# A bidirectional selective-scan block on one core: projections of each pass, once a phase of their own, spread in pieces over the scan of the pass before

## What is computed

```python
h, gate = adaln(x, cond)                  # layernorm, then (1 + scale) and shift from cond @ w + b
xs, z = split(h @ in_w)                   # 256 -> 2 x 512
xs = silu(xs)
proj = xs @ xproj_w                       # 512 -> 512 + 64 + 64
dt = softplus(proj[:512] + dt_bias); B = proj[512:576]; C = proj[576:640]
A = -exp(A_log)
for t in range(256):
    hst = hst * exp(dt_t[:, None] * A) + (dt_t * xs_t)[:, None] * B_t[None, :]
    y_t = hst @ C_t
ssm = (y + xs * D) * silu(z) @ out_w
x = x + gate * (ssm_fwd + ssm_bwd)
x = x + gate2 * (silu(h2 @ w1) * (h2 @ w2) @ w3)      # h2 = adaln(x) again
```

## Time and profile before

| | |
|---|---|
| median of 3 runs | 5650.15 us |
| the profiled execution, its own time | 5651.32 us |
| its span, first to last instruction | 5649.6 us |
| mean granted TensorE clock | 0.986 |
| busy: PE / DVE / ScalarE (ACT) / POOL | 80% / 86% / 56% / 57% |
| projections | 0 to about 656 us |
| first scan starts, last one ends | 690.7, about 5187.5 us |

### The profile page before, as it was taken

How to read it: one execution, slowest core, us unless ns; L and a number is a source line. 1 busy time by engine, 2 the same in 40 slices (tenths; PEclk the granted TensorE clock), 3 DMA queues, 4 the chain that set the end, 5 groups by cost and what they waited for, 6 DMA issues and landing times. The chain is left out here.

```text
span 5649.6 us, 129100 instructions
## 1 busy us (share of the span) xinstructions
PE 4528.9 (80%) x44208; PEld 2356.7 (42%) x44208; DVE 4867.9 (86%) x2556; ACT 3161.1 (56%) x10364; POOL 3230.3 (57%) x6078
## 2 busy tenths in 40 slices
PE   8999677777777777777777777777777777776898
PEld 4445344444444444444444444444444444443444
DVE  2332499999999999999999999999999999997433
ACT  4665466666665666665656565656565656564121
POOL 0000176767676767676767676767676767674221
PEclk9999899999999999999999999999999999998899
DMA  4333201111111111111111111111111111112551
GB/s 136 130 112 137 94 26 28 29 29 28 29 28 28 28 28 28 28 28 28 28 28 28 28 28 28 28 28 28 28 28 28 28 30 28 28 28 71 163 156 63
DMA packets 394408, 273.65 MB, mean 48 GB/s; under 512 B 212416, under 2 KB 299968, under 8 KB 393792
## 3 DMA queue, kind: packets, MB, share of 16 engines
q1 hardware_dynamic: 389568, 261.61, 15.4%
q10 hardware_dynamic: 4224, 4.19, 0.2%
HBM read 154.24 MB, written 111.41 MB: 47 GB/s over the span
## 5 line engine op out<-in xcount | busy, mean ns | idle before, releaser
L808 DVE TENSOR_TENSOR_SCAN b_hs<-b_dA,b_u 128x1024 f32<-128x1024 f32 x2048 | 4484.4, 2269 | 20.4 <-PE b_u L831 9.3
L831 PE MATMUL b_u<-b_ud,b_bw 32*128 32x256 f32 x16384 | 2322.9, 399 | 971.5 <-ACT b_dA L744 854.7
L744 ACT ACTIVATE b_dA<-b_ex 128x496 f32<-128x496 f32 x4096 | 2282.8, 585 | 257.0 <-PE b_ex L841 255.2
L841 PE MATMUL b_ex<-b_dd,b_aw 32*128 32x512 f32 x8192 | 2349.9, 641 | 28.8 <-DVE b_aw L796 28.1
L831 PEld LDWEIGHTS b_u<-b_ud,b_bw 32*128 32x128 f32 x16384 | 1489.9, 184 | 1941.7 <-issue 961.1
L655 POOL TENSOR_TENSOR b_dd<-b_dr,b_mask 128x512 f32<-128x512 f32 x1024 | 1073.4, 1048 | 1207.1 <-DVE b_hs L808 1188.7
L861 PE MATMUL b_y<-b_hs,b_cw 128*32 128x256 f32 x16512 | 1293.0, 390 | 2.7 <-DVE b_hs L808 2.7
L759 ACT ACTIVATE b_u<-b_hin 128x32 f32<-128x32 f32 x1792 | 362.7, 202 | 1502.7 <-PE b_u L831 939.7
L664 POOL TENSOR_TENSOR b_ud<-b_ur,b_mask 128x512 f32<-128x512 f32 x1024 | 1082.5, 1057 | 0.0
L841 PEld LDWEIGHTS b_ex<-b_dd,b_aw 32*128 32x128 f32 x8192 | 649.4, 183 | 30.8 <-issue 28.5
L743 ACT ACTIVATE b_first<-b_ex 128x16 f32<-128x16 f32 x3584 | 630.7, 176 | 38.5 <-PE b_ex L841 33.5
(11 more groups left out here) (98 smaller groups left out, 1918.2 us busy)
## 6 DMA issues: line engine op xcount, KB each, us to landing
scratch_y<-b_ysb SPq DMA_DIRECT2D x129, 256.0 KB, 2.1
b_u<-scratch_ut SPq DMA_DIRECT2D x256, 128.0 KB, 2.9
scratch_xs<-a_xs SPq DMA_DIRECT2D x16, 1024.0 KB, 7.2
scratch_sz<-a_sz SPq DMA_DIRECT2D x16, 1024.0 KB, 8.8
scratch_dt<-a_dt SPq DMA_DIRECT2D x16, 1024.0 KB, 4.5
scratch_ut<-a_uT SPq DMA_DIRECT2D x16, 1024.0 KB, 7.9
b_ur<-scratch_ut SPq DMA_DIRECT2D x1024, 16.0 KB
b_dr<-scratch_dt SPq DMA_DIRECT2D x1024, 16.0 KB, 1.7
```

Of the source, the lines that this page charges most:

```text
L744: nc.scalar.activation(dA[:, j % NDA, h, :, 1:TC], src[:, :, 1:TC], ACT.Exp).then_inc(exp_done, 1)
L808: nc.vector.tensor_tensor_scan(hs[:, c % 2, v, :, :, kp].rearrange("p d t -> p (d t)"), dA[:, j % NDA, :, :, :].rearrange("p h d t -> p (h ...
L831: ins = nc.tensor.matmul(dst[:, :, tb, :], bw[row(r), c % 2, tb, :], ud[row(r), j // 2 % NPR, tb, :, :], start=(tb == 0), stop=(tb == NTB ...
L841: nc.tensor.matmul(e[bank_of(p, 2 * j + h)][:, :], aw[row(r), d, v, :, :].rearrange("p b s -> p (b s)"), dd[row(r), j // 2 % NPR, :, :].re ...
```

## The change

The first two phases become one, `main_phase`. The work of one pass is now a `unit(q)`: a Python generator on each engine, cut into pieces, which yields after each. Unit 0 runs whole before the scan. Unit p + 1 runs during pass p: PE takes one piece after each step, ScalarE one piece in each step from j = 3 on, POOL two in each pair from the third on, SP one group of stores and loads after the loads of each chunk but the first. `wait_steps(n)` leaves n steps without a piece, and so lines the engines up.

- There are two PSUM banks for exponents instead of three (NDT), since one bank (b_job) is now for the units. PE's wait for the bank stands ahead of each exponent matmul instead of ahead of the step.
- The states hs have one buffer instead of two; the add-up goes by half chunks (8 steps), each in the 8 steps after it, and read_y comes twice as often with half the width.
- Silu is made of Exp, Ln and Exp on ScalarE (x * exp(-ln(1 + exp(-x)))) with a clamp and a product on POOL; softplus' four DVE operations become two on ScalarE and three on POOL, the product u one more on POOL; normalising goes to POOL, the root is Ln and Exp. All functions come from one table set, loaded once. Of the units only bn_stats and bn_aggr stay on DVE.
- B and C are projected in one job, and B is then transposed. Weights are held for one direction at a time, and are loaded anew for each pass.

The diff, cut to its core:

```diff
-        NDA, NPR, NM, NDT = 4, 4, 4, 3
+        NDA, NPR, NM, NDT = 4, 4, 4, 2
-        hs = sb("b_hs", [P, 2, SPN, SD, TC, 2])
+        hs = sb("b_hs", [P, SPN, SD, TC, 2])
+        GROUP_AT = {1: (0,), 2: (1,), 3: (2,), 4: (3, 4), 5: (5,), 6: (6,), 7: (7,)}
+        SILUS = 2 * JB
+        DT_JOB = (8, 10, 13, 15)
+        UT_JOB = (11, 14, 16, 17)
+        BC_JOB, BT_JOB, UNIT_JOBS = 9, 12, 18
+        STAT_AT = {64: 0, 66: 1, 68: 2, 70: 3}
+        AGGR_AT = {72: 0, 74: 1, 76: 2, 78: 3}
...
@@ SP @@
+                        load(p, c)
+                        if p + 1 < PASSES:
+                            if c == 1:
+                                side = unit(p + 1)
+                            if c:
+                                next(side)
...
@@ POOL @@
+                def softplus(q, j):
+                    m = q * JB + j
+                    pool.wait_ge(logged, m + 1)
+                    nc.gpsimd.tensor_tensor(nd[:, :], wy[:, :], ey[:, :], ALU.subtract).then_inc(nd_made, 1)
+                    yield
+                    pool.wait_ge(nd_made, 2 * m + 1)
+                    nc.gpsimd.tensor_tensor(nd[:, :], ln[:, :], nd[:, :], ALU.subtract).then_inc(nd_made, 1)
+                    yield
+                    pool.wait_ge(nd_made, 2 * m + 2)
+                    pool.wait_ge(sz_stored[j], (q + 1) * 16)
+                    nc.gpsimd.tensor_tensor(sd[:, j, :], pre[:, :], nd[:, :], ALU.add).then_inc(dt_made, 1)
+                    yield
+                    pool.wait_ge(dt_made, m + 1)
+                    if j >= 2:
+                        pool.wait_ge(full, first_job(q) + UT_JOB[j - 2] + 1)
+                    nc.gpsimd.tensor_tensor(us[:, j % 2, :], sd[:, j, :], xs[:, j, :], ALU.mult).then_inc(u_made, 1)
+                    yield
+                def unit(q):
+                    for i in range(SILUS):
+                        clamp(q, i)
+                        yield from wait_steps(3)
+                        if i:
+                            times_sigmoid(q, i - 1)
+                        yield
+                    yield from wait_steps(4)
+                    times_sigmoid(q, SILUS - 1)
+                    yield from wait_steps(2)
+                    for j in range(JB):
+                        yield from softplus(q, j)
+                        yield from wait_steps((8, 10, 8, 12)[j])
...
@@ POOL, one_pass @@
                         if c:
                             carry_in(p, 2 * i)
+                        if i >= 2:
+                            next(side, None)
                         ahead(p, i + 1, turn_u, last)
...
                         if c:
                             carry_in(p, 2 * i + 1)
+                        if i >= 2:
+                            next(side, None)
...
@@ ScalarE @@
+                def sigmoid(q, i):
+                    m = q * SILUS + i
+                    both = cl[:, i % 2, :]
+                    act.wait_ge(clamped, m + 1)
+                    nc.scalar.activation(both, both, ACT.Exp, scale=-1.0).then_inc(chain, 1)
+                    yield
+                    act.wait_ge(chain, 3 * m + 1)
+                    nc.scalar.activation(both, both, ACT.Ln, bias=1.0).then_inc(chain, 1)
+                    yield
+                    act.wait_ge(chain, 3 * m + 2)
+                    nc.scalar.activation(both, both, ACT.Exp, scale=-1.0).then_inc(chain, 1)
...
+                def take_dt(q, j):
+                    m = q * JB + j
+                    n = first_job(q) + DT_JOB[j]
+                    bias = dtb[:, q % DIRS, j:j + 1]
+                    act.wait_ge(full, n + 1)
+                    if m:
+                        act.wait_ge(dt_made, m)
+                    nc.scalar.activation(pre[:, :], job_bank(n)[:, :], ACT.Relu, bias=bias)
+                    nc.scalar.activation(ey[:, :], job_bank(n)[:, :], ACT.Abs, bias=bias).then_inc(freed, 1)
+                def log_part(q, j):
+                    m = q * JB + j
+                    act.wait_ge(freed, first_job(q) + DT_JOB[j] + 1)
+                    nc.scalar.activation(ey[:, :], ey[:, :], ACT.Exp, scale=-1.0).then_inc(bent, 1)
+                    yield
+                    act.wait_ge(bent, 2 * m + 1)
+                    nc.scalar.activation(wy[:, :], ey[:, :], ACT.Identity, bias=1.0).then_inc(bent, 1)
+                    yield
+                    act.wait_ge(bent, 2 * m + 2)
+                    nc.scalar.activation(ln[:, :], wy[:, :], ACT.Ln)
+                    nc.scalar.activation(wy[:, :], wy[:, :], ACT.Identity, bias=less[:, :]).then_inc(logged, 1)
...
+                def unit(q):
+                    for i in range(SILUS):
+                        take_xz(q, i)
+                        yield
+                        if i:
+                            yield from sigmoid(q, i - 1)
+                        else:
+                            yield from wait_steps(2)
+                        yield
+                    take_dt(q, 0)
+                    yield
+                    yield from sigmoid(q, SILUS - 1)
+                    yield
+                    yield from log_part(q, 0)
+                    take_bc(q)
+                    yield from wait_steps(6)
+                    take_dt(q, 1)
+                    yield
+                    yield from log_part(q, 1)
+                    yield from wait_steps(3)
...
@@ ScalarE, one_pass @@
                         if j >= STEPS:
                             put_carry(p, j)
+                        if j >= 3:
+                            next(side, None)
                         if j + 2 < JP:
                             decay(p, j + 2)
...
@@ PE @@
+                def project_xz(q, i):
+                    n = first_job(q) + i
+                    bank_free(n)
+                    for k in range(MB):
+                        ins = nc.tensor.matmul(job_bank(n)[:, :], win[:, k, i * P:(i + 1) * P], hT[:, q % DIRS, k, :],
+                                               start=(k == 0), stop=(k == MB - 1))
+                        if k == MB - 1:
+                            ins.then_inc(full, 1)
+                        yield
...
+                def unit(q):
+                    pe.wait_ge(win_loaded, (q + 1) * 16)
+                    pe.wait_ge(freed, turn_job(q // DIRS) + MB)
+                    for i in range(SILUS):
+                        yield from project_xz(q, i)
+                        yield from wait_steps(2)
+                    yield from project_dt(q, 0)
+                    yield from wait_steps(2)
+                    yield from project_bc(q)
+                    yield from wait_steps(2)
+                    yield from project_dt(q, 1)
+                    yield from wait_steps(2)
...
@@ PE, exponent and step @@
+                    pe.wait_ge(exp_done, exped_to(p, 2 * j + h - NDT))
...
                     for tb in range(NTB):
                         for h in range(2):
                             inject(p, j, h, tb)
                         if then:
                             exponent(*then, tb)
-                    for n_half in HALF_AT.get(k, ()):
-                        add_up(p, c, n_half)
+                    if half:
+                        for g in GROUP_AT.get(k % HALF, ()):
+                            add_up(half - 1, g)
...
                     for j in range(JP):
-                        step(p, d, j, nxt)
+                        step(p, j, last)
+                        next(side, None)
```

955 lines of the change are left out of this document (490 added, 465 removed).

## The result

The changed kernel takes 5967.1 us (median of 4 runs, 5954.8 to 5976.2) against 5650.4: a ratio of 1.056 (95% interval 1.0538 to 1.0581). I had forecast 5414, with 5210 to 5640 as range: wrong, in sign too.

A forecast was written before the change was run, and what follows sets the result against it. The scan instruction was taken to bind, with the PE-ScalarE loop equally long. 5651.3 - 581 (start) - 4 (end) + 348 (23.2 a pass x 15) = 5414 us; range 5210 to 5640.

The forecast's parts named there:

- Start, end: Before and after the scan: first scan at 110 instead of 690.68, -581 us; last add-up halved, -4 us.
- (a): Scan steps with one ScalarE piece between carry and exponentials: the piece fits, cost 0, steps stay 2.19 us.
- the loop has no room: Rival, scan: moved wait frees nothing, each ScalarE piece lengthens its step by 0.51; 5726 us, chance 0.12.
- (b): PE's pieces in scan steps: stalls in four xz jobs in carry steps, 3.6 us a pass; steps without carry 0.
- (d): POOL's softplus pieces in four steps running delay carries: 3.0 us a pass.
- 36 x 0.21: Drain rival: each of 36 PE pieces a pass pays a 0.21 us mode change on the path; 5510, chance 0.04.
- (c): ScalarE waits for a PE piece of the same step, five times a pass, holding the exponentials: 13.3 us a pass.
- (e): Small scan costs: transposes, ut, bt, PE mode changes 1.7; DVE statistics and two-piece modulation steps 1.6 us a pass.
- Both signs: Scans 2.5 or more apart beside a lone ScalarE piece refute (a); idle before scans over 585 us refutes the whole.

The follow-up runs named there:

- 5461 us kernel: Changed kernel with ScalarE's pieces and read of y behind the exponentials, POOL's pieces later and the double add-up at step 6: 5461.2 us.
- the better kernel: The 5461 us kernel; with PE's four injections put ahead of its two exponent matmuls it measured 5396.0 us, 65 less.

## Why the prediction was wrong, step by step

**Start, end.** Right: 115.95 for 110, and 3.7 for 4.

**(a) was the step that failed.** "The piece just fits into what the moved wait frees": it frees nothing. I counted only the injections behind the wait, 0.6, and left out the exponent matmul that stands ahead of them and is what the wait holds. Its two passes take 1.13 (177.71 to 178.84), and the carry starts 0.20 after them, as it does in 1614 of 1627 waits. That is 1.33 us, as long as from PE's start to the carry in a step before (3002.09 to 3003.43), although the wait now stands in another place. So each piece ahead of the exponentials costs its 0.5 where nothing else makes the step long. In the changed kernel that is 214 us, for which the sum had 0; all 60 pieces of a pass at full price would be some 460, but 21 steps hold a PE piece too, where the ScalarE piece adds 0.2, and the first steps of a pass have no carry. The rival "the loop has no room" named this mechanism and its evidence, that loop and scan are equally long, and I gave it 0.12. Its own price of 5726 is too low by 241: it has 465 us for the pieces, where 214 were measured, and nothing for (b), (d) and the rest, some 470.

**(b) was mis-sized.** The sum had 3.6 us a pass, on slack that isn't there, and two sizes too small. In a row of steps with nothing between on PE (the kernel with ScalarE's pieces behind):

```profile
1764.97 0.48 PE L968 MATMUL b_u<-b_ud,b_bw 32*128 32x256 f32 x2
...
1766.05 0.64 PE L998 MATMUL b_y<-b_hs,b_cw 128*32 128x256 f32 x8
...
1766.62 1.12 PE L887 MATMUL b_job<-b_xs,b_wxp 128*128 128x512 f32 x2
...
1767.68 0.48 PE L968 MATMUL b_u<-b_ud,b_bw 32*128 32x256 f32 x2
```

A step takes PE 1.65 and a piece 1.06, 2.71 together, where I had 1.5 and 0.88. Each step with a piece is then 0.52 over a scan, and most follow one another too closely to catch up. In one pass of that kernel (1368 to 1680 us) 36 steps with a PE piece, projections and transposes, and no same-step read are 20.7 us over 2.18, 0.57 each; in the 5461 us kernel it is 20.3 for 37 steps. So (b) is some 20 us a pass, 300 us in all, for 54. The run with 13 of 36 pieces gives less, 0.42 a piece, which for all 36 would be 227 us; the size lies between the two. The add-up of two groups beside a piece (17 us) is part of it. The steps without carry, for which I had 0, are 3.6 us a pass over.

By the Trainium skill, "TensorEngine Tiling (Array Packing)", Key Properties, a change of tiling mode drains TensorE; the trace agrees with it in so far as a piece takes 0.18 more than its two passes of 0.44. It was right to weigh it, and wrong to let only 36 x 0.21 hang on it: PE's whole row was over its limit, with or without the 0.18.

**(c) was right in size, in part by luck**: 200 forecast, 214 won by moving the reads. In the table above the five steps are 14.1 us a pass, where I had 13.3. But the scans came 2.2 to 3.6 late, not 1.7, and behind that the clock fell. From the rows at either level, a step of 3.62 in place of 2.67 loses 0.95, a quarter of its time. By that, an estimate, 240 us fewer at half clock are some 60 of the 214, and about as much stays when the reads stand behind (0.8 each, 75 of them).

**(d) matched by luck**: 45 forecast, and 51 won by moving POOL, but in the kernel with ScalarE's pieces behind, and not where I had looked: in the first 64 steps of a pass, nearly all in the first 48, which hold the clamps and products of the silu jobs, and not at the later softplus jobs. In the changed kernel itself the carry waits for POOL 163 times, 146 us in all, and mostly for the 0.84 that it waited in the step before; what POOL costs there is not shown.

**(e)** was not measured by itself. **A term that the list did not have** is the add-up of two groups. Before, it cost nothing, with 20 us of idle time in all. Now PE's row is full in a step without any piece: where the add-up started 1.09 after PE (3002.09 to 3003.18), it starts 1.60 after it, since the second exponent matmul waits for its own bank, and the double add-up makes the step 2.5 long. At 0.3 for each of 14 in a pass and 16 passes that is some 70 us, an estimate. No run tells apart here what the moved wait does and what the missing third bank does. The read of y, now twice as often ahead of the carry, costs next to nothing.

**The sum.** From 5651 - 585 = 5066, the change lost 901 us: 214 (a), 214 (c with the clock), some 300 (b), 51 (d), and some 120 that are left over, of which the double add-ups (70) and the same-step reads that still cost 0.8 each when they stand behind (60) are enough to fill it. These parts overlap, and they were won one behind the other in that order, so the last is a remainder and not a measurement. With (a) alone right, the forecast would still have been some 340 too low. The order of engines was followed through one kind of step at a time; the range took in neither two of my zeros being wrong together nor the clock. Both signs that I had named for it came: 2.65 between scans beside a lone ScalarE piece, and 818 us of idle time, over the 585.

What stays open: the clock's own price was read from rows and not isolated by a run, since no order tried here changed the clock and nothing else; what POOL's pieces cost in the changed kernel; and how much of PE's fuller row is the missing third bank.

## What to carry to other kernels

When a resource-bound loop is already closed through three engines, a piece put into it can cost its whole length however idle its engine is, and nothing a few instructions later in the same order (0.52 against 0.00 us here, for one move of two lines): find the place behind the instruction that others wait for. Add up the row of each engine for the fullest step, mode changes included, and compare that with the period before trusting averages such as "80% busy". When a matmul's result is waited for, count the matmuls ahead of it in the row to their ends, and put what others wait for first (184 us here, and 65 in the better kernel). Before blaming an instruction for a long step, check that the long step moves with it. When pieces of several engines hang on each other, moving one row moves the waits to the next engine, so move them together, and test the second limit with the first one removed.
